# A decoder layer's feed-forward: the clamp's difference computed on GpSimd, and another order of VectorE's operations in a unit

## What is computed

```python
def _qdot(x, w, out_dtype=BF16):
    return jnp.dot(x.astype(E4M3), w.astype(E4M3), preferred_element_type=out_dtype)
ff_gate = _qdot(x, w_gating[0])                 # x: 1792 x 256, w: 256 x 1024
gate_value = jax.nn.gelu(ff_gate)
ff1 = _qdot(x, w_gating[1])
activations = gate_value * ff1
outputs = _qdot(activations, w_linear)          # w: 1024 x 256
x = x + outputs                                 # its input was layernorm(x)
```

## Time and profile before

| | |
|---|---|
| median of 3 runs | 1716.51 us (1715.1 to 1719.35) |
| the profiled execution's own time | 1717.53 us |
| its span in the trace | 1715.2 us |
| busy over the span: TensorE, VectorE, ScalarE, GpSimd | 1561.6, 1402.8, 1122.1, 746.5 us |
| mean granted clock of TensorE | 0.959 |

### The profile page before, as it was taken

One profiled execution on the slowest core, in us unless ns is written; L12 is line 12 of the kernel. 1 busy time (PEld: TensorE's weight loads), 2 busy tenths in 40 slices (PEclk: granted clock), 3 DMA queues, 4 the chain that ended last, 5 costly groups with the idle time before them and its releaser, 6 DMA issues. The chain is left out here.

```text
span 1715.2 us, 45769 instructions
## 1 busy us (share of the span) xinstructions
PE 1561.6 (91%) x18290; PEld 1320.9 (77%) x18290; DVE 1402.8 (82%) x2513; ACT 1122.1 (65%) x2171; POOL 746.5 (44%) x727
## 2 busy tenths in 40 slices
PE   5899999998746999999999999999999999999455
PEld 5888888887535888888888888888888888888234
DVE  3788777787375889889899899898898898898687
ACT  3565555565344777777777777777777777777474
POOL 1566555565144344434434434444344354343014
PEclk9999999999677999999999999999999999999777
DMA  6000000000041111111111111111111111110001
GB/s 192 2 1 2 2 2 0 1 1 0 1 147 46 49 41 50 50 50 49 50 46 43 49 50 50 49 50 50 43 51 44 50 49 50 50 50 2 1 11 33
DMA packets 41613, 66.69 MB, mean 39 GB/s; under 512 B 7749, under 2 KB 40194, under 8 KB 41282
## 3 DMA queue, kind: packets, MB, share of 16 engines
q1 hardware_dynamic: 41410, 63.93, 12.9%
HBM read 62.08 MB, written 1.84 MB: 37 GB/s over the span
## 5 line engine op out<-in xcount | busy, mean ns | idle before, releaser
L1144 POOL TENSOR_TENSOR xa_CW<-xa_CTX,xa_CH 128x500 fp32r<-128x500 f32 x187 | 305.4, 1633 | 592.6 <-ACT xa_CH L1338 592.6
L1366 DVE TENSOR_TENSOR xl_ACC<-xl_ACC,xl_PB 125x896 f32<-125x896 f32 x320 | 438.3, 1370 | 11.0
L1330 ACT ACTIVATE xl_PB<-banks,xl_BIB,xl_SCB 125x896 f32<-125x896 f32 x384 | 401.0, 1095 | 32.1 <-PE banks L1202 31.7
L1357 DVE TENSOR_SCALAR xl_PB<-xl_PB 125x896 f32<-125x896 f32 x384 | 249.6, 650 | 64.1 <-ACT xl_PB L1330 63.0
L1312 ACT ACTIVATE xl_V<-banks 125x256 f32<-125x256 f32 x384 | 147.4, 384 | 155.3 <-PE banks L1169 155.3
L1169 PE MATMUL banks<-xa_WVhigh,xa_CH 128*125 128x256 f32 x768 | 238.6, 311 | 0.0
L1169 PE MATMUL banks<-xa_WVlow,xa_CH 128*125 128x256 f32 x768 | 216.0, 281 | 0.0
L1169 PE MATMUL banks<-xa_WVhigh,xa_CW 128*125 128x256 f32 x768 | 215.9, 281 | 0.0
L1303 ACT ACTIVATE xl_KXhigh<-banks,xa_bk 128x500 fp32r<-128x500 f32 x192 | 130.4, 679 | 100.4 <-PE banks L1169 100.4
L1218 PE MATMUL banks<-xl_PB,xl_V 125*32 125x112 f32 x6144 | 187.2, 262 | 1.5 <-DVE xl_PB L1357 1.5
L1373 DVE SCALAR_TENSOR_TENSOR xl_KXlow<-banks,xa_bk,xl_KXhigh 128x500 fp32r<-128x500 f32 x192 | 137.4, 715 | 55.0 <-ACT xl_KXhigh L1303 54.4
(11 more groups left out here) (234 smaller groups left out, 3954.6 us busy)
## 6 DMA issues: line engine op xcount, KB each, us to landing
xa_CTX<-in_ctxT SPq DMA_DIRECT2D x93, 500.0 KB, 3.6
fw_WO<-in_W_o SPq DMA_DIRECT2D x1, 2048.0 KB, 17.7
xq_WR<-in_w_gating SPq DMA_DIRECT2D x1, 2048.0 KB, 9.7
X<-in_x SPq DMA_DIRECT2D x1, 1792.0 KB, 10.2
out<-ff_R SPq DMA_DIRECT2D x16, 112.0 KB, 1.9
fw_QUT<-in_W_quT SPq DMA_DIRECT2D x1, 1536.0 KB, 12.5
xa_CTX<-in_ctxT SPq DMA_DIRECT2D x1, 1500.0 KB, 15.0
xq_WL<-in_w_linear SPq DMA_DIRECT2D x1, 1024.0 KB, 11.8
```

What stands on the lines that cost most here:

```text
L1144: nc.gpsimd.tensor_tensor(context_piece(CW, i), context_piece(CTX, i), context_piece(CH, i), ALU.subtract).then_inc(ctx_low, 1)
L1330: nc.scalar.activation(PB[t % PR][:, :, :], banks[0:TK, 2 * i:2 * i + KT, 0:QW], ACT.Exp, scale=SCB[j][:, t:t + 1], bias=BIB[j][:, t:t + 1 ...
L1357: nc.vector.tensor_scalar(pt, pt, E_HI, E_LO, ALU.min, ALU.max).then_inc(clipped, 1)
L1366: nc.vector.tensor_tensor(ACC[j][:, :, :], prev[:, :, :], PB[t % PR][:, :, :], ALU.add).then_inc(summed, 1)
```

## The change

GpSimd makes D8 (u = n - 2) in a loop over the units: it waits for `clamped`, and from the third unit on for `a_ready` of two units earlier, since D8 has two buffers, and then for its own result. The additions ff_R are put between: the one of the pair that `keep_output` took in unit n - 1 follows D8 of unit n - 2, and those of the remaining pairs come after the last D8. Each addition now waits for its own end as well.

VectorE's order in iteration n becomes: C of n - 2, PR of n, A of n - 3, T of n. A is thus made one unit later than before, and the loop is one iteration longer. A second wait for `half_ready` ahead of PR is gone. ScalarE, TensorE and SyncE keep their lists.

```diff
--- before.py
+++ after.py
@@ -1616,13 +1616,28 @@
 
             @block.gpsimd
             def _(pool):
-                for g in range(PAIRS):
+                def add_output(g):
+
                     it, p = g // PPS, g % PPS
                     pool.wait_ge(y_ready, g + 1)
                     if it:
 
                         pool.wait_ge(stored[p], it * 16)
                     nc.gpsimd.tensor_tensor(R[p][:, :], X[:, g, :], Y[g % 2][:, :], ALU.add).then_inc(r_ready, 1)
+                    pool.wait_ge(r_ready, g + 1)
+
+                for n in range(FF_UNITS + 2):
+                    u = n - 2
+                    if u >= 0:
+                        pool.wait_ge(clamped, u + 1)
+                        if u >= 2:
+                            pool.wait_ge(a_ready, u - 1)
+                        nc.gpsimd.tensor_tensor(D8[u % 2][:, :], H8[u % 2][:, :], C8[u % 2][:, :], ALU.subtract).then_inc(rest_ready, 1)
+                        pool.wait_ge(rest_ready, u + 1)
+                    if n < FF_UNITS and n and pair_after(n - 1) is not None:
+                        add_output(pair_after(n - 1))
+                for g in range(outputs_before(FF_UNITS - 1), PAIRS):
+                    add_output(g)
 
             @block.vector
             def _(dve):
@@ -1651,24 +1666,17 @@
                 for g in range(PPS):
                     rows(g)
                 widen(0)
-                for n in range(FF_UNITS + 2):
+                for n in range(FF_UNITS + 3):
                     u = n - 2
-                    if u >= 0:
+                    if 0 <= u < FF_UNITS:
                         dve.wait_ge(half_ready, u + 1)
                         nc.vector.tensor_scalar(C8[u % 2][:, :], H8[u % 2][:, :], FP8_MAX / 2, -FP8_MAX / 2, ALU.min, ALU.max).then_inc(clamped, 1)
                     if n < FF_UNITS:
                         i = n % 2
                         dve.wait_ge(up_ready, n + 1)
                         dve.wait_ge(gv_ready, n + 1)
-                        if u >= 0:
-                            dve.wait_ge(half_ready, u + 1)
                         nc.vector.tensor_tensor(PR_[i][:, :], GV[i][:, :], UP[i][:, :], ALU.mult).then_inc(prod_ready, 1)
-                    if u >= 0:
-                        dve.wait_ge(clamped, u + 1)
-                        nc.vector.tensor_tensor(D8[u % 2][:, :], H8[u % 2][:, :], C8[u % 2][:, :], ALU.subtract).then_inc(rest_ready, 1)
-                    if n < FF_UNITS:
-                        dve.wait_ge(prod_ready, n + 1)
-                        nc.vector.tensor_scalar(T8[n % 4][:, :], PR_[n % 2][:, :], FP8_MAX, -FP8_MAX, ALU.min, ALU.max, saturate=False).then_inc(t_ready, 1)
+                    u = n - 3
                     if u >= 0:
                         if u >= 2 * FT:
                             dve.wait_ge(y_done, (u // FT - 1) * PPS)
@@ -1676,6 +1684,9 @@
                         dve.wait_ge(t_ready, u + 1)
                         nc.vector.scalar_tensor_tensor(out=A8[(u // FT) % 2][:, u % FT, :], in0=D8[u % 2][:, :], scalar=2.0, in1=T8[u % 4][:, :],
                                                        op0=ALU.mult, op1=ALU.add).then_inc(a_ready, 1)
+                    if n < FF_UNITS:
+                        dve.wait_ge(prod_ready, n + 1)
+                        nc.vector.tensor_scalar(T8[n % 4][:, :], PR_[n % 2][:, :], FP8_MAX, -FP8_MAX, ALU.min, ALU.max, saturate=False).then_inc(t_ready, 1)
                     it, m = n // FT, n % FT
                     if it + 1 < SUP and m in ROWS_AT:
                         rows((it + 1) * PPS + ROWS_AT[m])
```

## The result

| | before | after |
|---|---|---|
| median of 8 runs | 1716.46 us (1714.99 to 1722.59) | 1723.49 us (1718.11 to 1724.95) |
| the profiled execution: time, span | 1717.53, 1715.2 us | 1724.1, 1722.2 us |
| GpSimd busy over the span | 746.5 us | 774.9 us |
| mean granted clock of TensorE | 0.959 | 0.956 |

The ratio after to before is 1.0033, with a 95% interval from 1.0018 to 1.0047: slower by 3.1 to 8.1 us. The time of 1723.5 us lies inside the stated range and 3.3 above the predicted 1720.2. The forecast of "within 0.3%" and "slower by over 0.3%", held at 0.52 and 0.40, are divided by a bound in the middle of that interval, so the runs do not choose between those two words. They do exclude a gain.

The account below looks back on a forecast made before the run. VectorE was taken to bound the feed-forward; D's 0.93 us on GpSimd would replace its 0.54 in VectorE's path. Unit and drain changes summed to +3.7 us, giving 1721.2 profiled and 1720.2 median, range 1714 to 1729.

Parts of the forecast that it names:

- the last part of the prediction: Signs in the trace: D shortest near 0.9 us, some PR, A or C 0.8 to 1.3, plain units 2.3 to 2.4.
- T is shut out by TF's example: VectorE's T and C, clamps like TF (stretched to 1.90 us in weight preparation), assumed to exclude GpSimd's operations too.
- the one for ff_Y: Units with keep_output: ff_Y on VectorE assumed to hide under GpSimd's turn, as ff_X does; such units took 2.31 us before.
- the slots showed no gap for the new order: VectorE's full units: distances between instruction starts showed no dependence gap, so the new order alone removes nothing.
- a step `rows` hides under GpSimd's turn: Units with rows: ff_X, stretched to 0.75 us, hides beside GpSimd's operation; units go from 2.30 to 2.27, -0.15 over five.
- a saving at the handover: VectorE and GpSimd taking turns: a handover between engines already waiting saves up to 0.20 us a turn.
- Plain units: Units n = 6 to 8, without side work: D waits until VectorE stops at A; 2.35 us for 1.98, +1.11 in all.
- the 0.05 that I read off the weight preparation: Handover from VectorE to GpSimd: D at 503.75 began 0.05 us ahead of the end of A's slot, 503.80.
- The second: Slower rival, VectorE and GpSimd turns: nothing saved at a handover, plain units 2.45 us; +7.3, 1723.8 us; chance 0.22.
- The third: Slower rival: D let in only where VectorE stops at A, side work stays on the path; 1729.1 us, chance 0.16.
- the first: Faster rival: VectorE and GpSimd overlap, ScalarE's 1.78 us bounds every unit; about -14, 1702.5 us; chance 0.08.
- The fourth: No-change rival: GpSimd let in with the full saving in every turn, plain units too; 1714.7 us, chance 0.08.

## Why the prediction came out as it did

**The mechanism was right.** Every stretched instruction that the last part of the prediction asked for is there: D at 982 ns at the shortest and 1303 in the mean, A up to 1.45, PR, C and T up to 0.86, 1.17 and 1.06, ff_X up to 1.07. Two of its signs did not come: plain units are at 2.23 and not at 2.3 to 2.4, and VectorE is not idle ahead of A in them. The assumption that T is shut out by TF's example holds. So does the one for ff_Y: it stays at 0.41 while D runs (n = 16, where the next C waits in its place, 0.84). The reading that the slots showed no gap for the new order holds too: 0.9999. The sum's sign was right, its size short by 2.6 us in the loop, 6.24 for 3.66.

**Steps that were mis-sized.**
- `rows` and `widen`: the step "a step `rows` hides under GpSimd's turn" was read off one C that followed an addition's end by 0.07 (1667.98 and 1668.05 in the earlier trace rows). That row was right, but I gave these units a saving at the handover on top, which belongs to a long operation that waits; ff_X held its place. 2.27 was taken, 2.43 measured, and 5.36 for 5.08. This term is wrong by +0.61 over five units (n = 19, shortened by the late D, is among them) and by +0.56 over n = 4 and 12.
- n = 20: the forecast listed that ff_R would stand ahead of D on GpSimd's queue and what waits behind ff_R, but priced the addition only by its length. Starved, it made D late and left VectorE with nothing to do: 1.45 us more than forecast (6.53 for 5.08). The sign was in the earlier trace rows, the addition that waited over nine microseconds; it had been booked as one that "cost nothing", which is true as long as nobody's D is behind it.
- Plain units: I assumed that D finds no opening until VectorE stops at A for want of it. D found it each time at the end of PR and A never stopped: 2.23 for 2.35, better by 0.34 over n = 6 to 8. What I assumed does happen, but only where C follows side work and no more of it comes: at n = 20, and at n = 27 of the runs with `rows` moved and with D alone on GpSimd. The saving was 0.13, T following D's end by 0.40 where A's slot is 0.53, and not 0.20; the 0.05 that I read off the weight preparation did not appear.
- n = 2: 1.80 was forecast and 2.04 measured. The forecast gave D no turn in this unit; T waited for it there (1.06). With D on VectorE the same order took 1.79.
- n = 14 and the end: the forecast took the granted clock as unchanged. The gap of 0.80 was taken as D's cover and no more, and the unit became shorter by 0.34, because TensorE's clock rose earlier. It is not that VectorE had less to do: in the run with the additions on VectorE and D there too, the unit took 2.32 at a granted clock of 1.00. The clock took back 0.44 over the last four outputs, so that the two nearly cancel; I count that as luck.
- The units with outputs and the drain came out within 0.3 of the forecast, group by group (15 to 18, 23 to 26, 27 to the end), and n = 22 at the edge of that (+0.26 for -0.04). The 2.84 that was taken for each unit of 15 to 18 and 23 to 26 is no unit's length, though: short ones of 1.77 to 2.43 stand beside long ones of 3.05 to 4.30, and only their sums are right.

**The rivals.** The second (nothing saved, 1723.8) names the measured time almost to the point, but not by its own steps: plain units did save something, and it had no late D. The third (2.78 with `rows`) did not occur. Nor did the first: beside a reading GpSimd neither PR nor A runs at 0.38 and 0.61, and what it would have been worth is shown by the run without D, 13 to 15 us. The fourth, 1714.7 with the full saving in every turn, is excluded by the interval, which begins 3.1 above the time before: plain units saved 0.13 of 0.20, and units with `rows` were longer than even the sum without a saving, 2.43 for 2.37.

## What to carry to other kernels

Before work is moved from VectorE to GpSimd, look in the trace for any instruction of either engine that is stretched while the other is busy: if it is, the moved work stays on the same path, at GpSimd's pace of 0.93 for 0.54 us here, and the free capacity in the table of busy shares is not there to be used. The reverse move is then worth a try: the additions, folded into a copy out of PSUM that VectorE made anyway, brought 6.3 us, some 2.6 of them by TensorE's clock in the executions that were profiled. And price an instruction on a starved queue by how long it may wait, times who stands behind it, not by its length.

## What the runs showed of the hardware that was not expected

- What GpSimd does decides whom it shuts out: a fill leaves PR and A at 0.38 and 0.61 and stretches T to 0.81 and one C to 1.12; a subtraction or an addition stretches all of them, and ff_X too. A copy out of PSUM keeps its 0.41 beside either.
- Who goes first does not follow from the moment at which D is issued. In plain units D begins 0.51 to 0.53 us after C and gets in ahead of A; at n = 3, 4, 10, 11 and 12 it begins 0.51 to 0.53 after C as well and waits for 1.83 to 1.85 (1636.45 to 1636.97, and 1645.90 to 1646.41, above). What goes along with it is the instruction ahead of C: where C follows ff_X or ff_Y without a pause, and D is issued as PR ends, A goes first; where C follows T, or VectorE was idle before it, D does. With `rows` behind the product, C follows T in n = 10 to 12, and D gets in at once (1.01). With T behind PR in place of A, D gets in everywhere. Why it is so was not tried.
- A single addition or difference that finds no opening can wait very long: before, one ff_R shows 10.33 us for 0.67 of work.
- TensorE's granted clock reaches into a feed-forward that VectorE bounds: the last four outputs took 3.67 us at 1.00 and 6.00 at a mean of 0.60.
- An engine that is shut out does not show as idle. Between 1636 and 1641 VectorE counts as busy throughout, although nearly 0.8 us of each A is waiting; the loss is seen in the mean durations alone.
